# Inverse square roots as powers on GpSimd, 64x64 score tiles, and a new order on TensorE and ScalarE

## The reference

```python
def l2norm(t):
    return t / jnp.maximum(jnp.linalg.norm(t, axis=-1, keepdims=True), 1e-12)

def attn_layer(x, Wqkv, qs, ksc, Wo):          # 16 heads of 64, window 32
    q, k, v = heads(x @ Wqkv)
    q, k = l2norm(q) * qs, l2norm(k) * ksc
    q, k = rotary(q, scale), rotary(k, 1 / scale)
    return merge(local_attention(q, k, v)) @ Wo  # softmax over own and previous window

def ffn_layer(x, g, bln, W1, b1, W2, b2):
    mu = x.mean(-1, keepdims=True)
    var = ((x - mu) ** 2).mean(-1, keepdims=True)
    xn = (x - mu) / jnp.sqrt(var + 1e-05) * g + bln
    a, gate = jnp.split(xn @ W1 + b1, 2, -1)
    return a * jax.nn.gelu(gate, approximate=False) @ W2 + b2

for i in range(DEPTH):
    x = attn_layer(shift_tokens(x), ...) + x
    x = ffn_layer(shift_tokens(x), ...) + x
```

## Time and profile before

| what | us |
|---|---|
| median of 3 runs | 4904.15 (4900.57 to 4906.8) |
| the profiled execution, its own time | 4893.89 |
| its span, from the first to the last instruction | 4892.1 |
| busy: PE, DVE, ACT, POOL | 3937.6, 3707.1, 3320.4, 2839.3 |
| granted TensorE clock, mean | 0.874 |

### The profile page before, as it was taken

One profiled execution on the slowest core, in us unless ns is written; L12 is line 12 of the kernel. 1 busy time (PEld: TensorE's weight loads), 2 busy tenths in 40 slices (PEclk: granted clock), 3 DMA queues, 4 the chain that ended last, 5 costly groups with the idle time before them and its releaser, 6 DMA issues.

```text
span 4892.1 us, 97213 instructions
## 1 busy us (share of the span) xinstructions
PE 3937.6 (80%) x24672; PEld 2525.8 (52%) x24672; DVE 3707.1 (76%) x12335; ACT 3320.4 (68%) x8937; POOL 2839.3 (58%) x4494
## 2 busy tenths in 40 slices
PE   4555548988888888788888888888888887888885
PEld 2223225655555555555555555555555555555553
DVE  7778768877777777677777777777777776777873
ACT  2222227878777777677777677786777776777774
POOL 2222237766566666566666566665666665666661
PEclk6555559999989999899999999999999998999997
DMA  1000012222222222222222222222222222222221
GB/s 40 4 4 2 4 58 92 85 79 85 83 85 76 81 82 85 79 83 81 80 80 85 83 85 75 82 82 86 86 75 85 75 90 79 86 79 78 86 71 58
DMA packets 225175, 351.70 MB, mean 72 GB/s; under 512 B 41534, under 2 KB 68348, under 8 KB 224380
## 3 DMA queue, kind: packets, MB, share of 16 engines
q1 hardware_dynamic: 224604, 345.22, 20.4%
HBM read 125.41 MB, written 5.77 MB: 27 GB/s over the span
## 4 chain that ended last, share of the span: by engine, by line
PE 39%; ACT 24%; DVE 12%; issue 10%; DMA 1%; ACTq 1%; POOL 0%; DVEq 0%; SPq 0%; POOLq 0%
ACT pr L745 11%; PE bank L279 6%; PE bank L583 5%; PE bank L594 5%; DVE sm L1106 4%; PE bank L281 4%; PE bank L280 4%; PE bank L551 3%; DVE ab L1060 3%; PE bank L564 2%; ACT L766 2%; PE bank L555 2%; ACT wide L754 2%; PE bank L565 1%; PE bank L537 1%
## 5 line engine op out<-in xcount | busy, mean ns | idle before, releaser
L745 ACT ACTIVATE pr<-sm,nb,rq 128x128 f32<-128x128 f32 (+1 forms) x3072 | 1520.4, 496 | 726.5 <-DVE nb L1112 704.7
L862 POOL TENSOR_SCALAR pr<-pr,rden 128x128 f32<-128x128 f32 (+1 forms) x3072 | 1133.4, 389 | 1259.8 <-DVE rden L1085 1258.9
L1060 DVE TENSOR_TENSOR ab<-bank,ltab 128x512 f32<-128x512 f32 x1536 | 985.4, 683 | 235.2 <-PE bank L281 208.0
L1106 DVE CUSTOM_DVE_ANT_0 sm<-bank,mask 128x128 f32<-128x128 f32 (+1 forms) x3072 | 844.8, 331 | 348.4 <-issue 296.5
L869 POOL TENSOR_TENSOR rot<-ab,swp 128x512 f32<-128x512 f32 x768 | 981.1, 1277 | 65.9 <-DMA swp<-ab 59.5
L733 ACT ACTIVATE sq<-bank 128x512 f32<-128x512 f32 x768 | 450.2, 586 | 262.6 <-DVE ab L1060 259.7
L564 PE MATMUL bank<-ident,pr 128*128 128x128 f32 x1536 | 439.1, 311 | 196.2 <-DVE pt L1092 195.7
L745 ACT ACTIVATION_READ_ACCUMULATOR pr<-sm,nb,rq 128x1 f32 x3072 | 575.6, 187 | 0.0
L551 PEld LDWEIGHTS bank<-rot 64*128 64x128 f32 x3072 | 241.1, 192 | 640.5 <-issue 436.2
L1092 DVE COPY pt<-bank 128x512 f32<-128x512 f32 x768 | 531.5, 692 | 10.3
L551 PE MATMUL bank<-rot 64*128 64x128 f32 x3072 | 392.0, 333 | 172.5 <-DVE nb L1112 151.1
(11 more groups left out here) (153 smaller groups left out, 7420.5 us busy)
## 6 DMA issues: line engine op xcount, KB each, us to landing
swp<-ab SPq DMA_DIRECT2D x1536, 128.0 KB, 2.0
rkb<-k_scratch SPq DMA_DIRECT2D x768, 128.0 KB, 2.9
raw<-Wqkv SPq DMA_DIRECT2D x48, 128.0 KB, 2.2
gg<-xT SPq DMA_DIRECT2D x48, 128.0 KB, 2.7
gg<-xT SPq DMA_DIRECT2D x48, 127.5 KB, 2.6
raw<-Wqkv SPq DMA_DIRECT2D x12, 256.0 KB, 2.8
wo<-Wo SPq DMA_DIRECT2D x6, 512.0 KB, 4.0
k_scratch<-rsum SPq DMA_DIRECT2D x192, 8.0 KB
```

The lines of the kernel that those rows point to most:

```text
L745: ins = act.activation(pr[:, s % 4, i, cs], sm[:, s % 2, i, cs], ACT.Exp, bias=nb[:, s, t, i:i + 1], scale=head_scale(rq, p, b)[:, t, i:i ...
L862: ins = pool.tensor_scalar(pr[:, e % 4, i, cs], pr[:, e % 4, i, cs], rden[:, e, t, i:i + 1], 1.0, ALU.mult, ALU.mult)
L1060: ins = dve.tensor_tensor(seqs(ab[:, j % 2, i, :]), seqs(use_bank("qk", j)[:, :]), ltab[:, 2 * (j % 2) + i:2 * (j % 2) + i + 1, :] .to_bro ...
L1106: ins = dve.tensor_tensor_reduce(sm[:, s % 2, i, cs], bank[i][:, cs], mask[:, cs], 1.0, -3e38, ALU.add, ALU.max, mx[:, t, i:i + 1])
```

## The change

Three powers a turn on GpSimd replace three Ln and three Exp on ScalarE. VectorE first brings the variance out of PSUM and adds the epsilon. Factors of a power of two (`KUP`, `R_LOG2`) that kept the logarithm accurate go. A score step becomes eight products of 64 queries with 96 keys, in four quarters of the array; what they leave unwritten of the banks is masked anyway and set to zero once. TensorE does in each step, behind the scores, first `dn`, `wo`, `rqT` and `cen` of the bank table and the output projection, then transposes, outputs and value projections, then the rest. ScalarE copies before its exponentials. Bank numbers, K scalings (four of them a step earlier) and the splitting of x (steps 11, 13 and 14) are set anew.

```diff
-BANK_STEPS = [[("next", "qk", 0, 4), ("prev2", "dn", 0, 5)],
+BANK_STEPS = [[("prev2", "dn", 0, 4), ("next", "qk", 0, 5)],
...
-SPREAD_STEPS = {0: ("cur", 3), 4: ("cur", 4), 5: ("cur", 5), 8: ("cur", 6), 10: ("cur", 7),
+SPREAD_STEPS = {0: ("cur", 3), 4: ("cur", 4), 5: ("cur", 5), 7: ("cur", 6), 9: ("cur", 7),
                 11: ("next", 0), 12: ("next", 1), 14: ("next", 2)}
-SCALE_STEPS = {13: [("cur", 7), ("next", 0)], 15: [("next", 1)], 1: [("cur", 2)], 3: [("cur", 3)], 7: [("cur", 4)],
-               9: [("cur", 5)], 11: [("cur", 6)]}
+SCALE_STEPS = {13: [("next", 0)], 15: [("next", 1)], 1: [("cur", 2)], 3: [("cur", 3)], 6: [("cur", 4)],
+               8: [("cur", 5)], 10: [("cur", 6)], 12: [("cur", 7)]}
+SCORE_TILES = [(0, 0, 0), (1, 32, 32), (2, P, P - WINDOW), (3, P + 64, P + 32)]
...
-                    for i in range(2):
-                        rows = slice(64 * i, 64 * i + 64)
-                        pe.matmul(bank[i][:, 0:P], rot[rows, p, c0:c0 + P], rot[rows, PAIRS + p, c0:c0 + P],
-                                  start=True, stop=True)
-                    for i in range(2):
-                        rows = slice(64 * i, 64 * i + 64)
-                        mm = pe.matmul(bank[i][:, P:UW], rot[rows, p, c0 + P:c0 + SEQ],
-                                       rot[rows, PAIRS + p, c0 + P - WINDOW:c0 + SEQ], start=True, stop=True)
+                    for half, c, k0 in SCORE_TILES:
+                        part = slice(64 * (half % 2), 64 * (half % 2) + 64)
+                        for i in range(2):
+                            rows = slice(64 * i, 64 * i + 64)
+                            mm = pe.matmul(bank[i][part, c:c + 96], rot[rows, p, c0 + 64 * half:c0 + 64 * half + 64],
+                                           rot[rows, PAIRS + p, c0 + k0:c0 + k0 + 96], start=True, stop=True)
...
                     if cur is not None:
                         scores(s)
+                    bank_work(s, ("dn", "wo", "rqT", "cen"))
+                    if s in (1, 2) and prev2 is not None:
+                        down(s, prev2)
+                    if WO_STEP <= s < WO_STEP + NWO and prev is not None:
+                        project_out(s - WO_STEP, prev)
                     if s < 3 and prev is not None:
                         transpose_probs(s + 13, prev)
...
+                    bank_work(s, ("qk", "g", "a", "var"))
                     if s in QUAD_STEPS and group_of(QUAD_STEPS[s][0], o) is not None:
...
                 for s in range(16):
-                    if cur is not None:
-                        probabilities(s)
                     if s % 2 == 0 and s < 6 and prev is not None:
                         copy_outputs(s // 2 + 5, prev)
...
+                    if cur is not None:
+                        probabilities(s)
...
-                    if s == 9 and (nxt is not None or prev is not None):
-                        norms(0, nxt, prev)
...
+                def inverse_root(h, q):
+                    ready = held(pool, n2 + (2 * q + h + 1))
+                    settle(pool)
+                    pool.wait_ge(sq_clamp, ready)
+                    pool.tensor_tensor(rsum[:, :], rsum[:, :], minus_half[:, 0:1].to_broadcast([P, GT]), ALU.pow).then_inc(r_inv, 1)
+
+                def inverse_deviation(q):
+                    ready = held(pool, n1 + (q + 1))
+                    settle(pool)
+                    pool.wait_ge(f_eps, ready)
+                    pool.tensor_tensor(xs, xs, minus_half[:, 0:1].to_broadcast([P, GT]), ALU.pow).then_inc(f_rstd, 1)
...
+                    if s == 2 and cur is not None:
+                        inverse_root(1, cur)
+                    if s == 9 and prev is not None:
+                        inverse_deviation(prev)
+                    if s == 9 and nxt is not None:
+                        inverse_root(0, nxt)
...
+                def spread_eps(q):
+                    dve.wait_ge(f_var, n1 + (q + 1))
+                    dve.tensor_scalar(xs, use_bank("var", 0)[:, :], 1e-5, None, ALU.add).then_inc(f_eps, 1)
...
-                    if gs[2] is not None and s == 8:
+                    if gs[2] is not None and s == 11:
                         if cur is not None:
                             dve.wait_ge(v_proj, n8 + 8)
                         split_high_x(gs[2], par)
-                    if gs[2] is not None and s == 9:
-                        split_low_x(gs[2], par, n1 + 3 if cur is not None else n1 + 2)
+                    if gs[2] is not None and s in (13, 14):
+                        split_low_x(gs[2], par, n1 + 3 if cur is not None else n1 + 2, s - 13)
```

More of the change, by code:

```diff
@@ L194, in build @@
         qk_proj, qk_sq, qk_mul, qk_rot = sem("qk_proj"), sem("qk_sq"), sem("qk_mul"), sem("qk_rot")
[L195 removed]
+        sq_part, sq_clamp, r_inv = (sem(n) for n in ("sq_part", "sq_clamp", "r_inv"))
         k_kept = sem("k_kept")
@@ L204, in build @@
         xs_in = sem("xs_in")
-        f_cen, f_sq, f_var, f_ln, f_rstd, f_xn, f_gb, f_hi, f_split = (
-            sem(f"f_{n}") for n in ("cen", "sq", "var", "ln", "rstd", "xn", "gb", "hi", "split"))
+        f_cen, f_sq, f_var, f_eps, f_rstd, f_xn, f_gb, f_hi, f_split = (
+            sem(f"f_{n}") for n in ("cen", "sq", "var", "eps", "rstd", "xn", "gb", "hi", "split"))
         f_g, f_gcp, f_gelu, f_a, f_h, f_dn, f_add = (sem(f"f_{n}") for n in ("g", "gcp", "gelu", "a", "h", "dn", "add"))
@@ L368, in keep_k_norms @@
                     used = held(sp_e, n8 + (8 * q + 4 * h - 4)) if prev is not None or (cur is not None and q == 1) else None
-                    sp_e.wait_ge(r_exp, norms)
+                    sp_e.wait_ge(r_inv, norms)
                     if used is not None:
@@ L495, in q_norms @@
                     settle(pe)
-                    pe.wait_ge(r_exp, norms)
+                    pe.wait_ge(r_inv, norms)
                     for t in range(4):
@@ L624, in down, with bank_work @@
                         mm.then_inc(f_dn, 1)
-                k = 0
+                def bank_work(s, whats):
+                    k = sum(len(step) for step in BANK_STEPS[:s])
+                    for b, (role, what, i, _) in enumerate(BANK_STEPS[s]):
+                        q = group_of(role, o)
+                        if what not in whats or q is None:
+                            continue
+                        free_bank(k + b)
+                        bk = use_bank(what, i)
+                        if what == "qk":
+                            project(i, q, bk)
+                        elif what == "rqT":
+                            q_norms(i, q, bk)
+                        elif what == "cen":
+                            centre(q, bk)
+                        elif what == "var":
+                            variance(q, bk)
+                        elif what in ("g", "a"):
+                            up(("a", "g").index(what), i, q, bk)
+                        elif what == "dn":
+                            down(0, q)
                 for s in range(16):
@@ L760, in copy_v @@
                                    bank[3][:, :].rearrange("p (t c) -> p t c", t=2), ACT.Copy).then_inc(v_sb, 1)
-                def norms(h, q, ln):
-                    if q is not None:
-                        act.wait_ge(sq_clamp, n2 + (2 * q + h + 1))
-                        act.activation(rsum[:, :], rsum[:, :], ACT.Ln, scale=float(2 ** R_LOG2)).then_inc(r_ln, 1)
-                    if ln is not None:
-                        act.wait_ge(f_var, n1 + (ln + 1))
-                        act.activation(xs, use_bank("var", 0)[:, :], ACT.Ln, bias=eps[:, 0:1]).then_inc(f_ln, 1)
-                    if q is not None:
-                        act.wait_ge(r_ln, n2 + (2 * q + h + 1))
-                        act.activation(rsum[:, :], rsum[:, :], ACT.Exp, scale=-0.5).then_inc(r_exp, 1)
-                    if ln is not None:
-                        act.wait_ge(f_ln, n1 + (ln + 1))
-                        act.activation(xs, xs, ACT.Exp, scale=-0.5).then_inc(f_rstd, 1)
                 def gate(c, q):
@@ L802, in turn @@
                         copy_v(V_STEPS[s][1], group_of(V_STEPS[s][0], o))
-                    if s == 2 and cur is not None:
-                        norms(1, cur, None)
+                    if cur is not None:
+                        probabilities(s)
                     if s == 7 and prev is not None:
@@ L1165, in turn @@
                         clamp(0, nxt)
+                    if s == 9 and prev is not None:
+                        spread_eps(prev)
                     if s == 3 and prev2 is not None:
@@ L1184, in turn @@
                         split_low(nl, 7)
+            for i in range(2):
+                dve.memset(bank[i][:, :], 0.0)
             dve.memset(xh[64:128, :, :, 0:1].bitcast(F32), 0.0)
@@ L1188, in _ @@
             split_high_x(0, 0)
-            split_low_x(0, 0, CREDIT + 1)
+            for half in range(2):
+                split_low_x(0, 0, CREDIT + 1, half)
             layer_tables(0)
```

78 lines of the change are left out of this document (29 added, 49 removed), and 2 rows, old and new, of the table BANK_STEPS.

## The result

| what | before | changed |
|---|---|---|
| median of the runs shown with the result (4 each) | 4902.67 | 16218.88 (16207.48 to 16233.37) |
| profiled execution, its span | 4893.89, 4892.1 | 16207.48, 16205.6 |
| granted TensorE clock, mean | 0.874 | 0.611 |

The ratio is 3.308, 95% interval [3.3023, 3.3137]. The forecast was 4544 us, the range up to 5010. The changed kernel takes 3.3 times as long.

What follows compares the result with a forecast made beforehand. TensorE was taken as nearest to full, its idle time partly waits through ScalarE's norm work. Gains of 8.2 - 2X + 1.35 + 1.9 + 1.62, or 7.5 us a turn, times 48 make 360 us: 4544 us, range 4390 to 5010.

Steps and rivals of the forecast that it cites:

- Step (2): GpSimd gets three powers of 128x512 a turn, each priced X = 2.8 us, between 1.28 and 7.7.
- C: GpSimd becomes the bound at steps 9 to 11; slower, 5043 us at X = 7, 5144 at 7.7; chance 0.17.
- (3): Path at steps 9 to 12: shorter by 8.2 - 2X us a turn, the power counting twice; 2.6 at X = 2.8.
- (4): Step 2: TensorE's 1.35 us of idle time goes; the power hides for some 5 us, beyond that costs X - 5.
- The constant 13.1: Gains in us a turn before the powers' price 2X is taken off: 8.2 + 1.35 + 1.9 + 1.62.
- X = 6.55: Price of a power in us where 13.1 = 2X, from which the change was to be slower.
- rival B: A dearer power on GpSimd, X of 3.8 to 6.5 us, still a gain: 4640 to about 4900 us; chance 0.20.
- rival E: Nothing moves: VectorE's own order (65.2 + 0.7 us) is the pace, idle time returns elsewhere; 4904 us; chance 0.04.
- Step (5): Score tiles: four quarters of the array run together, 0.16 us less a step over 12 steps, 1.9 us a turn.
- Rival D: Score tiles don't overlap: 12 steps lose 0.5 us each and the 1.9 is not won; 4923 us; chance 0.07.
- Step (6): Orders: ScalarE's copies ahead of its exponentials win 1.62 us a turn; TensorE's new order and earlier K scalings zero.
- Step (1): ScalarE loses six activations and four table loads a turn: 3.8 us at step 2, 5.0 at step 9.

Runs made afterwards that it cites:

- x1: Changed kernel with each power replaced by a product with 1 on GpSimd, constants for the norms: 4779.01 us, ratio 0.9745.
- v1: Changed kernel with each power on 32 of its 512 columns, a product with a constant on the other 480, bases constant: 5308.87 us, ratio 1.0832.
- x3: Kernel before with the 64x96 score tiles alone: 4874.17 us, ratio 0.9947.
- y4: Kernel before with 64x96 score tiles, norm activations replaced by a product with 1 on GpSimd, constant norms, old orders and tables: 4645.81 us, ratio 0.948.
- y3: x1 with both ScalarE's and TensorE's order within a step as before: 4638.3 us.
- y2: x1 with TensorE's order within a step as before, ScalarE's new order kept: 4594.45 us, ratio 0.9382.
- y1: x1 with ScalarE's exponentials back ahead of its copies, TensorE's new order kept: 4762.07 us.

## Why the prediction was wrong

**Step (2), the price X of a power**, failed, and with it the forecast: 2.8 us taken, 7.7 as the upper end, 81.9 measured. Passes over a tensor were the wrong measure: x1 shows that the same instruction with a product costs 1.04 us, so some 80.9 us are the function's. That no row showed the operation was said, yet nothing in the trace stood behind an upper end of six additions either. The Trainium skill's "GPSIMD Engine Reference" (section "Performance versus the Vector engine"), with an assumed 60 operations, gave an estimate of 8.5 us; measured is almost ten times that. The estimate pointed to the right side, and the chance of 0.17 for all of C was too small.

**Steps (3) and (4), how often X counts**, were right in the main. About twice up to 6.4 us (v1: 11.0 us a turn, 12.2 by its slopes) and three times beyond (3.01) is its 2X and X - 5. The full form, 18.1 - 3X a turn, with X = 81.93 gives 4894 + 227.7 x 48 = 15,823 us, within 2.4% of the profiled 16,207; the 8.0 us a turn that are missing are about what the constant was too large by in x1 (11.0 - 2.6 = 8.4).

**The constant 13.1** was too large; the break-even was therefore not X = 6.55. By the prediction's own step (4) it was not 6.55 either: beyond 5 us the sum is 18.1 - 3X, zero at 6.03, which rival B's "same formula" up to 6.5 leaves out. Term by term, in us a turn:

Steps (3) and (4), 8.2 - 2X + 1.35, at X = 1.04: 7.5 forecast, 4.8 measured (x3 to y4). The 8.2 set POOL's last step against a start of the up projection that POOL did not set. Before, the low half of xn was there 4.1 us ahead of the 2573.79 of the earlier trace rows (the clamp of step 9, then that half):

```profile
2554.75 0.69 DVE L1119 TENSOR_SCALAR rsum<-bank 128x512 f32<-128x512 f32 x1
...
2568.38 1.29 POOL L891 TENSOR_TENSOR xn_l<-gg,xn_h 128x512 fp32r<-128x512 f32 x1
```

From 2564.27 to 2573.79 TensorE was idle for 0.21 us in all and ran in part at half clock; it was late by the 3.50 us of the earlier trace rows, for VectorE's bias. What the powers could give back there is VectorE's wait for rstd:

```profile
DVE gg L1123 <- ACT gg L775: 162.0, 48, 10.6
```

That is 3.4 us each, less 0.69 for the epsilon; with the 1.35 of step 2 an estimate of 4.0 from these rows. In the turns shown, clamp to up projection went from 19.0 us (2554.75 to 2573.79) to 16.1 in y4: 3.0 less, where 8.2 - 2.1 = 6.1 was forecast. VectorE's wait for rstd goes, and its own order is what is left: in y4 it is busy 81% of the span, as much as TensorE. This is rival E in part.

Step (5): 1.9 forecast, 0.6 measured. The 0.21 a step was there (0.16 forecast); that 12 steps would pass it on was wrong, what arrives is the worth of 2 to 3, with longer waits and a lower granted clock beside it (x3). Rival D falls.

Step (6): ScalarE's new order 1.62 forecast, 0.9 measured with TensorE's old order (y3 to y2), and a loss of 0.4 with the new one (y1 to x1, 17 us, hardly more than the spread of their runs). TensorE's own new order "takes the same time as before, zero": measured a loss of 3.8, of which the centring product is 3.0. The prediction priced TensorE's moved work by its duration and never asked what the first instruction of the moved block waits for; a transfer that had been just in time at the end of the block was late at its head.

The measured terms, 4.8 + 0.6 + 0.9 = 6.3 a turn or 302 us, give 4598 us for y2, which takes 4594. That is no test: they are differences along one chain of runs (before, x3, y4, y3, y2), of which only the 8 us from y4 to y3 is left out.

**Step (1)** was right: the loads ahead of Ln and Exp are gone (L750 keeps 47, L777 48), and ScalarE's busy time fell by 393.6 us, 420 forecast. Of the signs of being wrong, X over 4 and a longer busy time of PE (3937.6 to 4003.4 us) came true, and PE's idle time at steps 9 to 12 grew (78.78 us ahead of one score product). The waits of PE for wide copies say nothing in a kernel that waits for powers; in x1 and y2 they are all but gone (under 2 us), as step (6) had it, but ScalarE's copies wait for PE instead.

## What to carry to other kernels

An operation that no row of the trace shows has no upper end until it has been run once: one run of the instruction by itself would have ruled this change out. Before work is moved ahead on an in-order engine, ask of its first instruction what it waits for, since that wait is then paid by all that it passed. When a function needs a table of its own, one activation between the two loads can be worth more than the activations that it saves (209 to 221 us here for 83.5 us of busy time): what others wait for comes after one load, and the way back is paid ahead of the work that needs it. Before two times are subtracted, ask whether the first was set by the chain that the second describes.
